# Layer 0 of a two-layer RWKV and latent-attention block: relu and exponentials alternate on ScalarE, rows are normalised at a chunk's end, and one rounding remainder moves behind another on VectorE

## What is computed

```
x    = L0_attn_x
xn   = layernorm(x)
r_in = xn*mix_r + prev*(1-mix_r)          # prev: xn of the token before; likewise k_in, v_in
receptance, key, value = r_in @ Wr.T, k_in @ Wk.T, v_in @ Wv.T
wkv  = a scan over tokens of (num, den, running max), with exponentials of key
s    = (sigmoid(receptance) * wkv) @ Wo.T
g    = silu(relu(xn @ W1 + b1) @ W2 + b2)
x    = x + s * g
```

## Time and profile before

| | us |
|---|---|
| median of 3 runs | 2026.55 (2025.97 to 2027.44) |
| the profiled execution | 2026.82 |
| its span, first to last instruction | 2025.1 |
| layer 0, all 16 chunks | from 0 to about 638 |
| first output projection (chunk 0) | 80.65 |
| that of chunk 14 | 596.50 |
| one chunk between them, (596.50 - 80.65) / 14 | 36.85 |

### The profile page before, as it was taken

How to read it: one execution, slowest core, us unless ns; L and a number is a source line. 1 busy time by engine, 2 the same in 40 slices (tenths; PEclk the granted TensorE clock), 3 DMA queues, 4 the chain that set the end, 5 groups by cost and what they waited for, 6 DMA issues and landing times. The chain is left out here.

```text
span 2025.1 us, 53401 instructions
## 1 busy us (share of the span) xinstructions
PE 1900.1 (94%) x22950; PEld 978.9 (48%) x22950; DVE 1729.8 (85%) x2249; ACT 1727.0 (85%) x2153; POOL 547.4 (27%) x426
## 2 busy tenths in 40 slices
PE   3999999999995999998999999999999999999986
PEld 1565565655653566664444443444434444344445
DVE  5999999999987788886888888888888888888878
ACT  5767867777666888886999999999999999999972
POOL 0564554655644666764000000000000000000004
PEclk9999999999997999998999999999999999999999
DMA  3001001001112356567221222222222222122129
GB/s 108 22 22 42 22 22 42 22 22 42 54 42 78 129 191 204 190 170 210 70 75 55 67 68 74 73 55 68 68 74 72 62 62 55 51 62 60 56 96 329
DMA packets 130220, 166.24 MB, mean 82 GB/s; under 512 B 13632, under 2 KB 101696, under 8 KB 129728
## 3 DMA queue, kind: packets, MB, share of 16 engines
q1 hardware_dynamic: 127952, 160.59, 26.5%
q10 hardware_dynamic: 2032, 2.24, 0.3%
HBM read 91.21 MB, written 71.57 MB: 80 GB/s over the span
## 5 line engine op out<-in xcount | busy, mean ns | idle before, releaser
L1757 ACT ACTIVATE c_probs<-c_ps_b 128x1536 f32<-128x1536 f32 x544 | 891.9, 1640 | 0.0
L1871 PE MATMUL c_ps_o<-c_probs,c_v 128*32 128x256 f32 (+3 forms) x6656 | 582.3, 453 | 3.9 <-DVE c_probs L1789 0.8
L1789 DVE TENSOR_SCALAR c_probs<-c_probs 128x2048 f32<-128x2048 f32 (+2 forms) x415 | 433.7, 1055 | 68.2 <-ACT c_probs L1757 67.8
L1851 PE MATMUL c_ps_b<-c_qk 24*128 24x256 f16 (+2 forms) x8064 | 459.9, 294 | 5.7 <-PEq L1094 5.7
L1851 PE MATMUL c_ps_a<-c_qk 24*128 24x256 f16 (+2 forms) x2688 | 449.9, 294 | 6.5 <-ACT c_probs L1756 4.9
L1756 ACT ACTIVATE c_probs<-c_ps_a 128x512 f32<-128x512 f32 x544 | 422.9, 777 | 2.5 <-PE c_ps_a L1851 2.4
L1851 PEld LDWEIGHTS c_ps_b<-c_qk 24*128 24x128 f16 x8064 | 222.8, 93 | 332.6 <-ACT c_probs L1757 243.9
L2022 POOL TENSOR_TENSOR d_prod<-d_prod,d_x 128x1024 f32<-128x1024 f32 x4 | 13.1, 3262 | 1029.4 <-DVE d_prod L2011 1029.4
L1871 PEld LDWEIGHTS c_ps_o<-c_probs,c_v 128*32 128x32 f32 x6656 | 161.7, 109 | 245.8 <-issue 126.9
L278 POOL TENSOR_TENSOR a_hidh<-a_hid,a_hidh 128x512 f16<-128x512 f32 x128 | 207.2, 1648 | 135.2 <-ACT a_hidh L404 134.0
L1794 DVE TENSOR_SCALAR c_probs<-c_probs 128x1536 f32<-128x1536 f32 (+2 forms) x208 | 165.6, 803 | 55.9 <-ACT c_probs L1757 53.6
(11 more groups left out here) (272 smaller groups left out, 2776.9 us busy)
## 6 DMA issues: line engine op xcount, KB each, us to landing
v_d<-b_val SPq DMA_DIRECT2D x16, 1024.0 KB
c_v<-v_d SPq DMA_DIRECT2D x64, 256.0 KB
rows<-in_x SPq DMA_DIRECT2D x16, 512.0 KB, 4.9
x_d<-rows_out SPq DMA_DIRECT2D x16, 512.0 KB, 3.3
rows<-x_d SPq DMA_DIRECT2D x16, 512.0 KB, 5.0
qc_d<-b_qc SPq DMA_DIRECT2D x16, 512.0 KB
kc_d<-b_kc SPq DMA_DIRECT2D x16, 512.0 KB
gate_d<-rows_out SPq DMA_DIRECT2D x16, 512.0 KB, 3.3
```

Of the source, the lines that this page charges most:

```text
L1757: nc.scalar.activation(probs[:, t % NPROB, PARTS[1]], ps_b[:, t % 2], ACT.Exp, scale=unscale).then_inc(exp_b_done, 1)
L1789: nc.vector.tensor_scalar(tile, tile, P_MAX, P_MIN, ALU.min, ALU.max).then_inc(clip_done, 1)
L1851: mm = nc.tensor.matmul(into, k[rows, hk, kt * P:(kt + 1) * P], tokens[rows, hq], start=(i == 0), stop=(i == len(TERMS) - 1), tile_positio ...
L1871: mm = nc.tensor.matmul(ps_o[j * VW:(j + 1) * VW, column:column + w], v[:, kt, j * VW:(j + 1) * VW], probs[:, step % NPROB, j, at:at + w], ...
```

## The change

Three pieces. (1) On ACT, relus and exponentials alternate: relu 0, new, relu 1, old, relu 2, relu 3, high half 0, bonus, relu 4 and so on, where before both state exponentials stood between relu 0 and relu 1 and the bonus one ahead of relu 2. (2) On ACT, `normalise` of chunk n+3 stands at the end of the queue of a chunk, behind the high halves of the mixed inputs, where before normalise of chunk n+2 stood behind the state copies; for chunk 1 it stands ahead of the conversion of the feed-forward and output weights. (3) On DVE, the second mixed_low, of the value input, stands behind rwkv's low half of the next body, where before it followed the first at once.

```diff
-                        normalise(n + 1, c + 1)
                         xn_of(n + 1, c + 1)
-                    hidden(n, 0)
-                    exponential(n, 0)
-                    exponential(n, 1)
-                    hidden(n, 1)
-                    exponential(n, 2)
+                    for m in range(2):
+                        hidden(n, m)
+                        exponential(n, m)
+                    hidden(n, 2)
...
-                    for m in range(2, MT):
+                    for m in range(3, MT):
...
                         hidden(n, m)
-                        if m in (2, 4, 5, 6):
+                        if m < MT - 1:
                             hidden_high(n, highs)
                             highs += 1
+                        if m == 3:
+                            exponential(n, 2)
...
                 act.wait_ge(scale_done, 2)
+                normalise(1, 1)
                 for i in (3, 4, 5):
                     weight_high(i)
...
                 mixed_high(1)
+                normalise(2, 2)
...
                         mixed_high(n + 2)
+                    if left >= 3:
+                        normalise(n + 3, c + 3)
...
-                def mixed_low(n):
-                    for m, i in enumerate(MIXED):
-                        dve.wait_ge(mix_high, len(MIXED) * n + m + 1)
-                        nc.vector.tensor_tensor(x_mix_half[i][:, 1], x_mix[m][:], x_mix_half[i][:, 0], ALU.subtract).then_inc(mix_low, 1)
+                def mixed_low(n, m):
+                    i = MIXED[m]
+                    dve.wait_ge(mix_high, len(MIXED) * n + m + 1)
+                    nc.vector.tensor_tensor(x_mix_half[i][:, 1], x_mix[m][:], x_mix_half[i][:, 0], ALU.subtract).then_inc(mix_low, 1)
...
-                mixed_low(1)
+                mixed_low(1, 0)
...
                     nc.vector.tensor_tensor(rwkv_half[:, 1], rwkv[:], rwkv_half[:, 0], ALU.subtract).then_inc(rwkv_low, 1)
+                    if left >= 1:
+                        mixed_low(n + 1, 1)
...
                         mix(n + 2)
-                        mixed_low(n + 2)
+                        mixed_low(n + 2, 0)
```

More of the change, by code:

```diff
@@ L640, in _ @@
                     weight_low(i)
-                mixed_low(0)
+                mixed_low(0, 0)
+                mixed_low(0, 1)
                 nc.vector.tensor_scalar(unscale[:, WR:VAL], power[:, WR:VAL], 1.0 / (F16_TARGET * XN_SCALE), None, ALU.mult).then_inc(bound_done, 1)
```

## The result

| | before | changed |
|---|---|---|
| median | 2026.93 (2025.97 to 2027.44, 4 runs) | 2009.45 (2008.53 to 2010.05, 4 runs) |
| profiled execution, its span | 2026.82, 2025.1 | 2009.66, 2007.9 |
| first output projection | 80.65 | 82.23 |
| that of chunk 14 | 596.50 | 578.47 |
| period | 36.85 | 35.45 |

The ratio is 0.9915, with an interval of 0.9901 to 0.9929: 17.5 us faster, where 2007.8 was forecast. The span lost 17.2: +1.6 at the start, -19.6 in fourteen periods, 0 in the last chunk, +0.8 behind it.

What follows compares the result with a forecast made beforehand. The prediction took a loop through DVE to bound the kernel. Per chunk -3.29 + 0.70 + 1.16 = -1.43, over fourteen periods -20.0, with +0.8 start and +0.5 allowance: 2008.1 profiled, 2007.8 median, range 2001.5 to 2019.

Steps and rivals of the forecast that it cites:

- DVE sets the period: Between output projections, 36.85 us: a closed loop through DVE sets the pace; PE only follows, so removing its two other waits gives nothing.
- Its loop: Output projection to L706 3.48, DVE without a pause to L693 29.66, then 3.71 to the next projection: 36.85.
- The second mixed_low: Moved behind rwkv's low half, it takes 3.29 off DVE's stretch and costs nothing there, covered by the 1.90 wait: -3.29 a chunk.
- First num scan: On DVE: POOL's first subtraction asks earlier, at 15.4, so this scan loses its turn: +0.70 a chunk, bounds -0.16 to +1.7.
- First mixed_low: At the chunk's end on DVE: it waits behind POOL's numerator L284, 2.84 to the next start instead of 1.68: +1.16 a chunk.
- Turn-taking: DVE and POOL instructions with two SBUF inputs wait whole instructions for whichever asked first; 1.09 behind on DVE, about 1.0 on POOL.
- The rival with statistics: Statistics on DVE queue with POOL's gate product, L706 starts 1.57 later: period 37.0, time 2029.5; chance 0.03.
- Start: Before the first projection: normalise of chunk 1 ahead of the weights costs 1.9, the subtraction that leaves gives 1.13: +0.8.
- End: In the last chunk PE waits for POOL's subtractions, whose turns DVE's scans set, not ACT: 0, within 0.7.
- The allowance of 0.5 for L708: 0.5 taken off the whole gain, since L708's turn may now meet the small row operations on POOL.
- Idle ahead of rwkv's high half: On ACT: normalise fits the idle time, leaving about 0.9; rival that ACT becomes late: 2035, chance 0.04.
- PE's need: What PE wants per chunk: 35.0 with its waits gone or shorter, plus 0.3 for relu 4, below the forecast period of 35.42.

Runs made afterwards that it cites:

- run 24: Not a run's number: kernels that execute all 24 receptance matmuls, unlike the two with the weights' low half left out, 16 matmuls, measured at 2006.13 and 2036.07.

## Why the prediction was right

- **DVE sets the period.** Right for both kernels. Three things show it: on the kernel before, both ACT edits took two of PE's waits, 0.98, and gave 0.28; PE 1.73 shorter left the changed kernel's period at 35.44; and its loop closes without slack by its rows, 28.25 on DVE from L713 to rwkv and 7.21 from rwkv back to L713, 35.46. (That starts add up to a period is so by itself; what counts is that each row starts at the end of the one that it waits for.) Its loop, though, ran through the output projection, which is not in it; the sum came out the same, since the projection and the gate chain both follow rwkv at a fixed distance. And it needed the ACT edits to hold: with the new DVE order and the old relu order PE sets the period, at 35.80.
- **The terms.** The second mixed_low left whole, -3.29: it runs in 1.22 at its new place and L713 starts 3.49 after the projection (3.48 before). First num scan: POOL asked at 15.36 (forecast 15.4) and L578 began at 20.04 (forecast 20.06). First mixed_low: 2.88 from start to start (forecast 2.84). The stretch came out as 28.25, forecast 28.23. Period 35.45 for 35.42.
- **Turn-taking.** The rule that the sum used held in every kernel. Of the DVE instructions of layer 0 with two inputs in SBUF (scans, products, sums, subtractions, between 80 and 600 us), 960 over the fourteen kernels start beside a running POOL product or subtraction, and all of them end 1.08 to 1.14 behind its end; the 1264 others take 1.21 to 1.29. For the first mixed_low that is 1.21 with no neighbour, 1.77 behind one POOL subtraction, 2.96 behind the numerator, 3.35 for a numerator behind it. The rival with statistics fell: in the changed kernel four of them took 1.40, as before, beside a gate product of 2.36. Of the page cited in the prediction, the Trainium skill, GPSIMD Engine Reference, Key points, only the part on two SBUF inputs shows in this trace.
- **Start.** The copies cost 1.97 (forecast 1.9), the subtraction that left gave 1.15 (forecast 1.13): +0.82 for +0.8. The first projection was another 0.76 late, and by that the forecast missed 81.4. This lies ahead of every edit: the first 24 receptance matmuls, begun at 28.35 and 28.10, took 6.68 in the kernel before and 7.70 in the changed one, and 6.7 to 8.2 over all kernels here that run 24. The first seven follow each other at 0.43 in the kernel before, the first eleven in the changed one, and the rest at 0.22, the spacing at full clock.
- **End.** 34.41 for 34.39, as forecast.
- **The allowance of 0.5 for L708** was not needed: its line (L715 now) took 1.22, and POOL's small L273 paid, 1.22 in place of 0.20 or so, with nobody waiting.
- **ACT.** Idle ahead of rwkv's high half 0.99, forecast 0.9.
- **PE's need.** Forecast 35.0 plus 0.3 for relu 4. The 0.3 is there, too short for a bracket: the first matmul of block 6 starts 0.50 after the one ahead of it instead of 0.22, and block 4 loses another 0.08. The whole came out as 35.16 for 35.3, and in the changed kernel POOL's low halves add 0.2, which the forecast did not have.
- Of the difference of 1.5 between the forecast of the span (-18.7) and the measured one (-17.2), 0.8 is the start ahead of the edits, 0.8 lies behind the last projection, 0.4 are the periods, and -0.5 is the allowance.

The forecast said nothing about which edit brings what. The runs do: the DVE edit two thirds, the two ACT edits the rest, and those almost only together and only beside it; on the kernel before they bring 0.28 a chunk, which the start takes back. One part of the change, normalise of chunk 1 at the start, is a loss.

## What to carry to other kernels

When two engines are both nearly full, find the one whose waits are a closed loop: start at one instruction, follow what releases what until it comes round, and check that no piece starts later than what it waits for allows. Do it again after each edit: here the loop of DVE held at 36.85, PE's wait for a relu at 35.80 and DVE again at 35.45. An edit off that loop gives nothing, even if it removes waits of the busiest engine, but it may shift who asks first for a shared resource, so sum it together with the others. A move into a wait is free only as far as the wait and its neighbours reach, here to within 0.05 us of POOL's next product; and what is right in the loop should be priced apart at the start, where there may be no idle time to cover it.

## What the runs showed of the hardware

- A third less work in one projection made the kernel before slower by 9 us: PE idles 2.1 ahead of 24 matmuls, and in nine chunks of fourteen these are granted 0.62 of the clock and take 4.45 instead of 2.78. With 1.65 idle it was in none. Behind the 2.51 of the last projection it was in nine kernels of fourteen, 1.4 to 1.7 us each, so a difference of that size between two kernels is not the edit's until this projection has been looked at.
- DVE and POOL take turns by whole instructions in the order in which they ask, when both have their inputs in SBUF. The profile shows the wait inside the second one's own busy time, not as idle time ahead of it. The second ends 1.1 behind the first on DVE (960 cases), 2.2 for a 128x1024 product on POOL (84 cases). Being second costs up to the neighbour's length: 2.96 instead of 1.21 on DVE behind a 128x1024 product, 3.3 instead of 2.36 for that product on POOL.
- The same first 24 matmuls took between 6.7 and 8.2 us from kernel to kernel, without any difference in what goes ahead of them, by how many of them follow at 0.43 before the spacing falls to 0.22: a microsecond at the start says nothing about an edit, unless it is counted from the second sums on.
